# Four graph layers on one core: the plain stage as a pipeline over six successive quads

## The reference

```python
h = relu(layernorm(x)); x = x + gcn2(h)            # W1 128x256, relu, W2 256x128
h = relu(layernorm(x)); x = x + sage2(h)           # twice: mean @ wl + bl + x @ wr, relu
h = relu(layernorm(x)); x = x + gine3(h, edge_attr) # three layers with edge features
h = relu(layernorm(x)); x = x + gat4(h)            # four attention layers, 2 heads of 64
```

## Time and profile before

| | |
|---|---|
| device time, median of 3 runs | 5651.72 us (5638.97 to 5663.69) |
| profiled execution: time, span | 5637.92 us, 5636.2 us |
| busy PE, DVE, ACT, POOL | 4057.7, 3541.7, 2667.5, 3543.3 us (72, 63, 47, 63% of the span) |
| mean granted TensorE clock | 0.897 |
| DMA | 971.59 MB, 172 GB/s in the mean |

### The profile page before, as it was taken

One profiled execution on the slowest core, in us unless ns is written; L12 is line 12 of the kernel. 1 busy time (PEld: TensorE's weight loads), 2 busy tenths in 40 slices (PEclk: granted clock), 3 DMA queues, 4 the chain that ended last, 5 costly groups with the idle time before them and its releaser, 6 DMA issues. The chain is left out here.

```text
span 5636.2 us, 116803 instructions
## 1 busy us (share of the span) xinstructions
PE 4057.7 (72%) x27481; PEld 3359.2 (60%) x27481; DVE 3541.7 (63%) x12527; ACT 2667.5 (47%) x6624; POOL 3543.3 (63%) x4145
## 2 busy tenths in 40 slices
PE   3777777777779777988899988866676576570076
PEld 2555555555558655767788877755675575560065
DVE  5666666666666687668666669933753763676533
ACT  2555555555544343346666668832232232230086
POOL 2544545444457675767675757457777777687577
PEclk9888888888889888999999999989899899795599
DMA  2444444444445686778543436578479479579543
GB/s 72 153 151 155 151 146 155 149 157 151 148 128 149 173 227 185 208 205 248 150 119 95 118 107 175 158 224 273 111 219 283 115 189 284 146 188 394 197 133 108
DMA packets 1087196, 971.59 MB, mean 172 GB/s; under 512 B 113214, under 2 KB 845974, under 8 KB 1087036
## 3 DMA queue, kind: packets, MB, share of 16 engines
q1 hardware_dynamic: 992956, 805.13, 46.0%
q0 software_dynamic: 94080, 164.48, 12.0%
HBM read 488.42 MB, written 484.70 MB: 173 GB/s over the span
## 5 line engine op out<-in xcount | busy, mean ns | idle before, releaser
L1092 POOL DMA_INDIRECT G<-table,idx_all x1568 | 1545.9, 986 | 739.5 <-issue 499.0
L1092 POOL DMA_INDIRECT G<-table,idx_l x588 | 607.0, 1032 | 289.6 <-issue 178.0
L1042 POOL DMA_INDIRECT XIN<-in_x,idx_x x196 | 188.4, 961 | 696.3 <-ACT GN L2168 575.4
L1763 PE MATMUL PS<-ident,G 128*128 128x128 f32 x1372 | 246.2, 292 | 356.5 <-ACT G L2168 326.4
L1763 PEld LDWEIGHTS PS<-ident,G 128*128 128x128 f32 x1372 | 161.0, 146 | 471.2 <-issue 418.3
L1766 PE MATMUL PS<-G,S 128*128 (+1 forms) x2352 | 408.5, 292 | 26.3 <-DMA G<-table,idx_all 15.8
L2168 ACT ACTIVATE G<-G 128x128 f32<-128x128 f32 x784 | 323.1, 482 | 171.9 <-DVE G L1307 109.9
L1766 PE MATMUL PS<-UT,w 128*128 128x512 f32 x492 | 377.1, 911 | 13.1 <-ACT UT L2168 12.1
L1766 PE MATMUL PS<-CR,LO 97*128 97x128 f32 x2352 | 336.1, 288 | 68.1 <-ACT CR L2168 68.0
L1766 PEld LDWEIGHTS PS<-G,S 128*128 128x128 f32 x2352 | 353.8, 204 | 45.8 <-issue 28.3
L1766 PEld LDWEIGHTS PS<-S,G 128*128 128x128 f32 x1960 | 256.4, 196 | 172.8 <-issue 157.4
(11 more groups left out here) (379 smaller groups left out, 10911.0 us busy)
## 6 DMA issues: line engine op xcount, KB each, us to landing
table<-G SPq DMA_DIRECT2D x392, 256.0 KB, 2.8
table<-RO SPq DMA_DIRECT2D x271, 260.0 KB, 3.3
table<-RO SPq DMA_DIRECT2D x245, 256.0 KB
XIN<-xrows SPq DMA_DIRECT2D x196, 256.0 KB
table<-OWN SPq DMA_DIRECT2D x147, 260.0 KB, 4.0
OWN<-table SPq DMA_DIRECT2D x139, 256.0 KB, 3.3
F<-table SPq DMA_DIRECT2D x132, 256.0 KB, 3.4
S<-table SPq DMA_DIRECT2D x100, 260.0 KB
```

What stands on the lines that cost most here:

```text
L1042: g.indirect_dma_start(M[:, j, :], None, x, bass.IndirectOffsetOnAxis(ap=idx_x[:, t:t + 1], axis=0)).then_inc(gat[j].sem, 16)
L1092: g.indirect_dma_start(G[:, t, 0:w], None, TAB[s], bass.IndirectOffsetOnAxis(ap=idx[:, t:t + 1], axis=0)).then_inc(gat[t % 4].sem, 16)
L1763: return nc.tensor.transpose(o, i, ident[0:k, 0:k])
```

## The change

Each engine's `plain` is written in a new order, and its operations refer to quads up to five back (q5) where they went to three back (q3). The first stretch stays on q0 and q1. The second stretch's transposes and `sampled` stay on q2, but `rows_a`, `rows_b`, `residual`, `constant` and the statistics of the third stretch go to q3; the rest of the third stretch goes to q4 and q5. On VectorE the second stretch's statistics, inverse and shift go from q1 to q2, the first's shift from q0 to q1. Waits follow the new order in four places: `rA` comes ahead of `rB`; `turned(q, 3)` waits for the copy of the attributes on even quads instead of odd ones, which is that of the same body; `attributes` on TensorE waits for `gT` of two quads before. `LAGS`, the bodies of the tail, is 5 instead of 3. No operation, shape, buffer or transfer is added or taken away.

```diff
-               2: lagged("q_p2", ("gT", "h2", "rB", "rA")),
+               2: lagged("q_p2", ("gT", "h2", "rA", "rB")),
...
-        LAGS = 3
+        LAGS = 5
...                                          (SP)
-                load_x(q0)
-                keep(q1, "t1", q_a[1], "g", PG[1])
-                keep(q2, "t3", q_a[2], "g", PG[2])
-                keep(q3, "x3", q_v[2], "xc", PX[3])
-                keep_x_norm(q3)
-                keep_x(q1)
-                keep(q1, "t2", q_a[1], "t1", PR[2])
-                next_attributes(q0)
-                keep(q2, "t4", q_a[2], "rA", PR[4])
-                keep_attributes(q2)
-                keep(q3, "t8", q_v[3], "r8", PR[8])
+                keep(q2, "t1", q_a[1], "g", PG[1])
+                next_attributes(q1)
+                keep(q4, "t3", q_a[2], "g", PG[2])
+                keep_attributes(q5)
+                keep_x(q2)
+                keep(q3, "t2", q_a[1], "t1", PR[2])
+                keep(q5, "x3", q_v[2], "xc", PX[3])
+                keep_x_norm(q3)
+                load_x(q0)
+                keep(q4, "t4", q_a[2], "rA", PR[4])
+                keep(q5, "t8", q_v[3], "r8", PR[8])
...                                          (VectorE, the new order)
+                shift(q1, 1)
+                stats(q2, 2)
+                rows(q5, 8)
+                aggregate(q2, 2)
+                aggregate(q4, 3)
+                x_stats(q1)
+                x_shift(q2)
+                stats(q0, 1)
                 with_bias(q1)
+                inverse(q4, 3)
+                attributes(q3)
                 aggregate(q0, 1)
+                inverse(q2, 2)
                 hidden(q1)
+                shift(q2, 2)
+                residual(q3)
+                x_aggr(q1)
+                normed(q4)
+                constant(q3)
+                convolved(q1)
+                x_inverse(q1)
                 inverse(q0, 1)
+                stats(q3, 3)
...                                          (TensorE)
-                if k == 3 and q[2]:
+                if k == 3 and not q[2]:
                     alone(pe, (e_cp, turn_of(q) + 1))
...
-                ready(pe, (q_a[3], earlier(q, 1), "gT"))
+                ready(pe, (q_a[3], earlier(q, 2), "gT"))
...
+                rows(q5)
+                attributes(q3)
                 turned(q1, 1)
-                turned(q2, 2)
+                rows_a(q3)
                 hidden(q1, 0)
                 hidden(q1, 1)
+                rows_b(q3)
+                convolved(q1)
+                turned(q2, 2)
+                turned(q4, 3)
                 sampled(q2)
-                turned(q3, 3)
-                convolved(q1)
-                attributes(q2)
-                rows_b(q2)
-                rows_a(q2)
-                rows(q3)
...                                          (ScalarE, the new order)
+                rows_a(q3)
+                norm(q2, 2)
+                root(q0, 1)
+                x_root(q1)
                 turned(q2, 2)
+                turned(q4, 3)
+                convolved(q1)
                 sampled(q2)
                 norm(q0, 1)
+                turned(q0, 1)
+                root(q3, 3)
                 root(q1, 2)
+                x_norm(q1)
+                hidden(q0)
```

More of the change, by code:

```diff
@@ L786, in plain @@
             def plain(m, b):
-                q0, q1, q2, q3 = (earlier((m, 0, b), k) for k in range(4))
-                load_x(q0)
-                keep(q1, "t1", q_a[1], "g", PG[1])
-                keep(q2, "t3", q_a[2], "g", PG[2])
-                keep(q3, "x3", q_v[2], "xc", PX[3])
-                keep_x_norm(q3)
-                keep_x(q1)
-                keep(q1, "t2", q_a[1], "t1", PR[2])
-                next_attributes(q0)
-                keep(q2, "t4", q_a[2], "rA", PR[4])
-                keep_attributes(q2)
-                keep(q3, "t8", q_v[3], "r8", PR[8])
+                q0, q1, q2, q3, q4, q5 = (earlier((m, 0, b), k) for k in range(6))
+                keep(q2, "t1", q_a[1], "g", PG[1])
[6 more added lines that the diff above has]
+                keep_x_norm(q3)
+                load_x(q0)
+                keep(q4, "t4", q_a[2], "rA", PR[4])
+                keep(q5, "t8", q_v[3], "r8", PR[8])
             load_attributes(0)
@@ L1401, in plain @@
             def plain(m, b):
-                q0, q1, q2, q3 = (earlier((m, 0, b), k) for k in range(4))
-                inverse(q3, 3)
+                q0, q1, q2, q3, q4, q5 = (earlier((m, 0, b), k) for k in range(6))
+                shift(q1, 1)
[6 more added lines that the diff above has]
+                stats(q0, 1)
                 with_bias(q1)
-                normed(q3)
-                stats(q0, 1)
+                inverse(q4, 3)
+                attributes(q3)
                 aggregate(q0, 1)
-                x_stats(q1)
+                inverse(q2, 2)
                 hidden(q1)
-                inverse(q0, 1)
-                x_aggr(q1)
-                shift(q0, 1)
-                convolved(q1)
-                attributes(q2)
[L1415 to L1425, removed]
+                shift(q2, 2)
[5 more added lines that the diff above has]
+                x_inverse(q1)
+                inverse(q0, 1)
+                stats(q3, 3)
             plain_stage(dve, plain)
@@ L2246, in plain @@
             def plain(m, b):
-                q0, q1, q2, q3 = (earlier((m, 0, b), k) for k in range(4))
-                turned(q1, 1)
+                q0, q1, q2, q3, q4, q5 = (earlier((m, 0, b), k) for k in range(6))
+                rows_a(q3)
+                norm(q2, 2)
+                root(q0, 1)
+                x_root(q1)
                 turned(q2, 2)
-                hidden(q1)
+                turned(q4, 3)
+                convolved(q1)
                 sampled(q2)
-                turned(q3, 3)
-                x_norm(q2)
-                root(q0, 1)
                 norm(q0, 1)
-                convolved(q1)
-                x_root(q1)
-                rows_a(q2)
+                turned(q0, 1)
+                root(q3, 3)
                 root(q1, 2)
-                norm(q1, 2)
-                root(q2, 3)
+                x_norm(q1)
+                hidden(q0)
             act.wait_ge(pd.sem, pd.at(0, 0))
```

## The result

The median is **5239.52 us** (5224.85 to 5249.23, 4 runs) against 5646.36 us (5638.97 to 5663.69, 4 runs) before: a ratio of **0.9276, 95% interval 0.9262 to 0.9289**, 406.8 us saved, where the prediction said 5250, 402 under the 5651.72 that it knew. The profiled execution took 5249.23 us (span 5247.5), the slowest of its four; that of before, 5637.92, lies under all four of its runs, so the two traces show only 388.7 us of it.

What follows compares the result with a forecast made beforehand. It took one loop of waits through TensorE's order to bound the kernel. 97 quads at 11.1 instead of 15.28 us save 405, less 5 for drain: 5238, or 5250 us as a median; range 5185 to 5430.

Steps and rivals of the forecast that it cites:

- The sum: Whole kernel: 97 periods shortened from 15.28 to 11.1 us, less 5 us, giving 5238 us against the profiled execution.
- T: Period of one quad in the plain stage, put at 11.1 us, forecast range 10.4 to 12.
- The drain: End of the plain stage: two more bodies to empty the pipeline, put at 5 us, between nothing and 20.
- The slow rival: TensorE at half clock throughout the new order binds at about 18.5 us a quad: 317 us slower, 5965 us; chance 0.06.
- (a): VectorE's own order binds: 10.0 us work, 0.2 load wait, 0.9 other waits, 11.1 us a quad.
- (b): Round of the x rows through GpSimd, VectorE and ScalarE, once in two quads: period at least 10.3 us, nearly binding.
- (c): TensorE's bank of the first stretch, from copy to final add: 8.2 or 9.2 us, not binding.
- (d): TensorE's work in sum: 9.8 us a quad at the full clock level, not binding.
- SP's order: Load of x moved to ninth place: SP already waits when x is free; a later load delays VectorE one for one.
- GpSimd as the bound: Plain stage: GpSimd, slowed by sharing VectorE's port, or transfers bind at 11.9 to 12.9 us a quad; chance 0.15.
- The low clock as the bound: TensorE staying at granted level 0.5 in the new order, about 18.5 us a quad, 5965 us; chance 0.06.
- These waits are one loop: Kernel before: ScalarE's normalisation, TensorE's turn and next hidden products, VectorE, convolution and back form one 15.76 us round.

Runs made afterwards that it cites:

- experiment 1: The changed kernel with VectorE's x_stats(q1) moved behind with_bias(q1) instead of ahead of x_shift(q2): 5218.34 us, ratio 0.9245 to the kernel before.
- experiment 2: The changed kernel with an extra GpSimd memset of about 1 us ahead of each pair's gathers of x rows: 5252.87 us, ratio 0.9312.
- experiment 5: The changed kernel with load_x(q0) last in SP's order, behind the stores t4 and t8, instead of ahead of them: 5484.54 us, ratio 0.9721.
- experiment 3: The kernel before with five unread products added on TensorE in each body, ahead of the second transposes, to hold up its clock: 5611.89 us, ratio 0.994.
- experiment 8: The kernel before with SP issuing the load of x one body ahead, behind the store t2: 5592.48 us, ratio 0.9911.
- experiment 9: The kernel before with the load of x behind the store t2, and two ScalarE roots ahead of long activations: 5542.52 us, ratio 0.9816.
- experiment 4: The kernel before with the second stretch's transposes behind the next quad's hidden products on TensorE, and their copy likewise on ScalarE: 5813.43 us, ratio 1.03.

## Why the prediction was right, and where it was not

*The sum.* T was put at 11.1 and measured 11.13; the sum against the profiled execution said 5238 where it took 5249.23. The drain was put at 5 us and came to 2; a start 5.4 us later and 6.7 us behind the stage were not in the sum. (The slow rival's 317 us on top of 5651.7 make 5969 us, not 5965; nothing hangs on it.)

*(a) VectorE: right in sum, wrong in its parts.* Predicted 10.0 of work, 0.2 for the load, 0.9 of other waits; measured 9.73 and 1.40, of which 0.02 for the load (0.7/35.9) and nothing at line 1348, whose wait had been the model for the 0.9. The idle time is 0.64 for the x rows, 0.45 at line 1368, 0.17 at 1354, 0.11 at 1342. Work came out 0.27 lower, waits 0.30 higher, and these two errors cancelled: that T was met within 0.03 us is luck. The forecast's 10.4 to 12 doesn't hang on it.

*(b) The x rows: the near-bound was real, but its round was mis-sized.* It was put at T of at least 10.3. The statistics followed the gather by 7.92 us instead of 7.1, and the gather's start followed the shift at 710.60 by 3.92 instead of 1.2 + 1.65 + 0.3: 11.84 us from shift to statistics, where 10.25 had been put. It fits into two periods only because from there to the next shift pass 9.87 us (722.44 to 732.31) and not a whole period, as the prediction had it: the body with the wait is the longer one of the two. That makes it VectorE's largest wait. GpSimd's wait for the normalisation fell from 12.0 to 22.7/18 = 1.26 us a pair, as said (under 3). By experiments 1 and 2 the round still is only one of several limits.

*(c), (d) TensorE: right.* 9.89 us busy against 9.8, clock 1.00, hidden products from 3.25 to 1.94 us (somewhat over half).

*SP's order: right.* SP stands waiting when the buffer comes free, and the price of a later load was nearly one for one: 2.94 us of wait, 2.52 of period in experiment 5.

*GpSimd as the bound: not seen.* Busy 269.79/35.9 x 2 = 15.0 us a pair against 14.8 before (241.62 over 16.4 pairs), with VectorE busy 87% instead of 66%. The lock that the Trainium skill describes (SBUF — State Buffer, "SBUF: two separate sides") agrees with single issues of 1.40 us; as a price for the loop it did not show. Nor did a busier VectorE meet it oftener: of 115 issues with indices before (600 to 900 us) 10 took over 1.15 us, all beside lines 1336 and 1317; of 161 after (500 to 800 us) 8 did. The low clock as the bound was not seen either.

*The step that failed is the account of what held the kernel before:* "These waits are one loop", through TensorE's order and its fallen clock. Holding the clock up gave 0.27 of the 4.15 us a quad (experiment 3). The loop has a link from the hidden products to VectorE's half, and there the kernel before waits 1.4 us of 500. From two of its bodies, SP, VectorE and ScalarE on the timeline:

```profile
816.08 2.20 SPq L745 DMA_DIRECT2D table<-G  x2
...
817.07 0.70 DVE L1368 COPY G<-PS 128x520 f32<-128x520 f32 x1
...
823.54 0.86 DVE L1378 BATCH_NORM_STATS2 stat<-XIN 128x6 f32<-128x128 f32 x4
...
839.88 0.69 ACT L2168 ACTIVATE G<-PS,b1l 128x512 f32<-128x512 f32 x1 [2.21 <-PE PS L1766]
...
840.95 1.64 ACT L2168 ACTIVATE GN<-XIN,nb,rs 128x128 f32<-128x128 f32 x4
842.49 0.28 ACT L2168 ACTIVATE G<-G,eps 128x4 f32<-128x4 f32 x1
...
842.80 0.18 DVE L1301 RECIPROCAL G<-G 128x4 f32<-128x4 f32 x1 [3.34 <-ACT G L2168]
```

In the round of the earlier trace rows the hidden products were done at 819.55 + 3.25 = 822.80, and VectorE's half began at 824.32, in order behind two sets of statistics, of which the first had waited 1.41 us for its load (822.27). That load, issued at 818.47, stands in SP's order behind the store of t8, and this behind VectorE's copy of 817.07. So this body's round goes through SP and the load. In the next body VectorE waits 3.34 us for a root (842.80) that stands in ScalarE's order behind the x rows' normalisation (840.95), and this behind the copy of `sampled`, which waited 2.21 us for TensorE (839.88): here the hidden products, ahead of `sampled` in TensorE's order, do lie on the way.

What stands in the loop's place: VectorE's in-order body held several round trips to other engines, with little of its own work between the asking and the using (roots of ScalarE, the load through SP, products of TensorE). Experiments 8 and 9 show that these waits carry part of the time and pass from one to the next: taking the load's alone gave 0.50 of 1.2 us a quad, easing the roots as well 1.04 in all. The change does not put a body between all of them, but it puts other quads' work there. Counted in VectorE's calls, from each `aggregate` to its `inverse`, with the root between, stood two, and now nine, eight and four; from `hidden(q1)` to `convolved(q1)` three, now five; from the call that lets the load go (`rows`, now `convolved`) to its statistics three, now ten. In its trace the waits are gone. How much of the gain each stretch brings is not shown: experiments 5 and 8 part the load from the rest, but no run lengthened the pipeline for one stretch only, and none took both ties of experiment 4 away by themselves.

## What to carry to other kernels

When no engine of a loop is near full, list for the engine with the most work each wait for a round trip to another engine, count how much of its own work stands between request and use, and put work of other iterations there for all of them together: the two that were eased alone here passed more than half of their idle time on. A link of a supposed loop counts only where an engine waits at it, and an edit that is to take it away has to do so in the order of every engine that holds it. Then look at the queue that issues the loads, since a load behind a store whose rows come late can give back more than half of such a gain. When the largest waits left are of like size and less work on any one engine returns next to nothing, the single edit is spent.

## What the runs showed of the hardware that was not expected

The granted clock did not rank the kernels. It was 0.79 in experiment 4, which is slower than the kernel before, 0.89 in that, 0.94 in experiment 5 (500 to 900 us) and 1.00 after; but in experiments 8 and 9, both faster than the kernel before, it was lower than there, 0.84 and 0.86:

```profile
600.00:1100.00 500.00, 391.96 (x2055) 271.86 (x2056) 337.83 (x1491) 295.35 (x694) 244.69 (x392) 0.84 0.48 156
```

```profile
600.00:1100.00 500.00, 393.71 (x2139) 279.42 (x2138) 351.76 (x1568) 306.06 (x717) 273.91 (x424) 0.86 0.49 164
```

Raised by itself to 0.98 it was worth 37 of the 407 us. GpSimd's issues with indices did not get dearer in the mean beside a busier VectorE: 986 ns in the stretch after, 994 before, though those for the x rows did (1007 and 959).
